# Two attention entrances of a four-block network: SyncE issues the row and stack transfers ahead of the queued DRAM writes

## The chip, the cores and the metric

The kernel runs on one core of a Trainium2 chip. The core has TensorE (PE, matrix products), VectorE (DVE), ScalarE (ACT), GpSimd (POOL) and SyncE (SP), which in this kernel does nothing but issue DMA transfers and wait for semaphores. The metric is the device time in microseconds (us) of one execution, lower is better.

## The reference, cut to what matters

```python
x = x + 0.5 * _L0_ffn_ref(_layernorm(x), ...)       # per-feature hidden layer of 16
x = x + _L0_attn_ref(_layernorm(x), ...)            # 16 heads of 8, banded bias, softmax
x = x + 0.5 * _L0_ffn_ref(_layernorm(x), ...)
x = x + 0.5 * _L1_ffn_ref(_layernorm(x), ...)       # fp4 quantised gated layer
x = x + _L1_attn_ref(_layernorm(x), ...)            # 16 causal heads over a latent of 64
x = x + 0.5 * _L1_ffn_ref(_layernorm(x), ...)
```

x is 8 batches of 256 positions by 128 features, float32. Each attention needs, for each batch and head, a 256 x 256 matrix of scores q k^T, its softmax, and the product with v.

## The kernel before, in words

Everything runs as six phases one after the other, on five instruction streams. Each stream's order is written out by hand (function `program` calls the steps), and semaphores join the streams. The change lies in the two **entrances**, the stretches where a projection phase (`proj_phase`) goes over into an attention phase (`attn_phase`): at about 40 to 90 us for the first layer's attention, and 276 to 325 us for the second layer's.

**The projection** works in four units (`p0` to `p0 + 3`), each for two batches. Per unit, q and k are split into bf16 parts (ACT lines 485 and 499, VectorE 492 or 494, GpSimd 503), and `sp_save` writes them from the tiles `q_parts` and `k_parts` to DRAM: three transfers for each of the two batches, six issues per unit, 1 MB. Semaphores `p_dram<unit><batch>` count their landing.

**The attention** works in 16 **units** of its own, each for eight heads of one batch: four slots make a quad, and a quad is two batches. So quad 0 reads what projection unit 0 wrote, quad 1 what unit 1 wrote, and so on. There are four stack buffers `qst[slot]` and `kst[slot]`. A unit needs

- its **stack**: `sp_stack` reads q and k parts back from DRAM in six issues (lines 641 and 642), and waits ahead of that until TensorE is done with the buffer (semaphore `a_t`);
- its **row**: VectorE finds the row maxima of the unit's scores, GpSimd splits them, TensorE turns them over (line 748), ACT copies them to `nmT` (line 801), and `sp_rows` copies `nmT` into the stack with one issue (line 653). The row comes with the maxima, so that the second, **shifted** pass over the scores (lines 693 to 701, in the second layer 703 and 704) gives score minus maximum.

The work is staged over units. In the unit of slot s, TensorE computes the shifted scores of s, and the plain scores of slot s + 2 (lines 672 and 673, in the second layer 675 to 679), whose maxima are wanted two units later; it starts the unit with the first pair of these plain scores. SyncE issues in the same unit the stack of slot s + 3 and the row of slot s + 1. TensorE takes its instructions in the order in which they are written. Idle products on `identb` (line 660) fill TensorE in the entrance.

In the entrance, `prefetch` issues the stacks of slots 0, 1 and 2 of quad 0, `front(0)` and `front(1)` make the scores, maxima and rows of slots 0 and 1, and `quad(0)` then runs the first four units. SyncE's order in all this is what the change rewrites. `saved(unit)` in `quad` has SyncE wait for the landing of a projection unit's writes. Stack 3 of quad 0 reads projection unit 0 only.

Of the kernel before, what the change touches and what calls it, by code (L numbers as in the profile page):

```python
# [58 lines left out]
def build(nc, A, out_d):  # L59
# [10 lines left out]
    with ctx:  # L70
# [382 lines left out]
        def proj_phase(inst, nu0, tu0, x_ready, entry, q_ready, k_ready, between):  # L453
# [147 lines left out]

            def last_save(sp):
                sp_save(sp, p0 + 3, 1)

            return dict(pe=pe_body, act=act_body, dve=dve_body, pool=pool_body, sp=sp_body, first=p0, n=4, entry=entry, ahead=ahead, last_save=last_save, opening=opening)


# [14 lines left out]

        def attn_phase(inst, last_save):
            l0 = inst == 0
            q0 = 4 * inst
# [258 lines left out]
            def unit(eng, which, qd, slot, has_prev, has_prev2, has_1, has_2, has_3, extra=lambda point: None):  # L884
# [5 lines left out]
                if which == "sp":  # L890
                    if has_3:
                        sp_stack(eng, *n3)
                    if has_1 and has_prev:
                        sp_rows(eng, *n1)
# [98 lines left out]
            def front(eng, which, slot):  # L993
# [23 lines left out]
                if which == "sp":  # L1017
                    sp_rows(eng, q0, slot)
                if which == "act":
                    act_maxT(eng, q0, slot)  # L1020
# [5 lines left out]
            def quad(eng, which, n, beside, loop=lambda qd, slot, point: None, final=lambda slot, point: None):  # L1026
# [4 lines left out]
                if n == 0:  # L1031
                    for slot in range(4):
                        unit(eng, which, q0, slot, slot > 0, slot > 1, True, True, True)
                        if slot == 0 and which == "sp":
                            last_save(eng)
                elif n == 1:
# [693 lines left out]
        def biases(eng, which):  # L1730
# [20 lines left out]
            if which == "pool":  # L1751
# [11 lines left out]
                            lambda dve, k: ffn_a["x"](dve, 2 + k, k) if k < 2 else None)  # L1763
        attn_a = attn_phase(0, proj_a["last_save"])
        ffn_b = ffn_phase(1, 8, 8, lambda t: ("a_y", 2 * (t + 1)),
# [9 lines left out]
                            lambda dve, k: step(dve, "dve", fp4_a, 15) if k == 1 else None)  # L1775
        attn_b = attn_phase(1, proj_b["last_save"])
        fp4_b = fp4_phase(1, 24, lambda t: ("a_x", t + 1),
# [3 lines left out]
        def program(eng, which):  # L1781
            def run(ph, lo, hi):
                for k in range(lo, hi):
                    step(eng, which, ph, k)
# [45 lines left out]
            def entrance(ph, at):  # L1830
# [3 lines left out]
                at["prefetch"](eng, which)  # L1834
                run(ph, 3, 4 if which == "sp" else 5)
                if which in ("pe", "dve"):
# [3 lines left out]
                elif which == "sp":  # L1840
                    at["front"](eng, which, 0)
                    run(ph, 4, 5)
                    at["front"](eng, which, 1)
                    run(ph, 5, 6)
                else:
# [197 lines left out]
```

## Time and profile before

| | us |
|---|---|
| median of 3 executions | 462.82 |
| lowest, highest | 458.14, 462.89 |
| the profiled execution, its time | 460.4 |
| its span in the profile | 458.4 |
| TensorE busy | 413.9 (90%) |
| VectorE busy | 348.8 (76%) |
| GpSimd busy | 298.3 (65%) |
| ScalarE busy | 284.8 (62%) |
| mean granted TensorE clock | 0.981 of full speed |

The span is the part of the execution that the profile covers from its first to its last instruction; 2.0 us of the execution's time lie around it. Times in the rows below count from the start of the span. In rows of SyncE ("SPq") the second number is how long the issue took on SyncE, not the transfer. The engines overlap, so their busy times don't add up to the span.

### The profile page before, as it was taken

The numbers are of one execution on the slowest core, as the hardware profiler recorded it, in microseconds if no ns is written. First come the engines' busy times: TensorE is split into PE (matmuls) and PEld (weight loads), VectorE is DVE, ScalarE is ACT, GpSimd is POOL, SyncE is SP. The second block draws the span as 40 slices with busy tenths as digits, with TensorE's granted clock in tenths as the row PEclk, the third lists the DMA queues.
The fourth block names the chain that finished last, engine by engine and source line by source line (L and its number), as shares of the span: only waits on it lengthen the run. The fifth ranks groups of instructions, "written<-read, shape, count | busy, mean of one in ns | idle before, by whom it ended". The sixth has DMA issues, their size and how long they took to land.

```text
span 458.4 us, 11229 instructions
## 1 busy us (share of the span) xinstructions
PE 413.9 (90%) x3804; PEld 265.9 (58%) x3804; DVE 348.8 (76%) x878; ACT 284.8 (62%) x523; POOL 298.3 (65%) x569
## 2 busy tenths in 40 slices
PE   8999789999999998897879888899999999887996
PEld 3555436666666654454447564567667766544674
DVE  5878766888778766996699986767788878367992
ACT  5886424666676676687886448055547575777732
POOL 5523625777777772357899647245676789779962
PEclk9999988999999999899899999989999999999999
DMA  7001876323224100000000006983343332000001
GB/s 215 2 1 49 203 211 166 107 77 85 88 73 104 55 4 1 2 0 2 0 1 2 1 1 165 234 224 93 80 104 107 82 80 56 5 0 1 23 24 46
DMA packets 31123, 31.82 MB, mean 69 GB/s; under 512 B 4953, under 2 KB 26329, under 8 KB 31074
## 3 DMA queue, kind: packets, MB, share of 16 engines
q1 hardware_dynamic: 31074, 31.18, 25.6%
q8 instruction: 28, 0.46, 0.4%
q14 instruction: 21, 0.17, 0.1%
HBM read 21.30 MB, written 9.44 MB: 67 GB/s over the span
## 4 chain that ended last, share of the span: by engine, by line
PE 49%; DVE 18%; POOL 15%; issue 8%; ACT 8%; DVEq 0%; POOLq 0%; ACTq 0%
PE psum L722 6%; ACT h_sb L349 4%; DVE nm L821 4%; POOL hq L1496 3%; PE psum L672 3%; PE psum L675 3%; PE psum L703 3%; PE psum L693 2%; PE psum L673 2%; POOL hb_v L1491 2%; PE psum L726 2%; DVE xn L240 2%; PE psum L694 2%; PE psum L660 2%; DVE nm L824 2%
## 5 line engine op out<-in xcount | busy, mean ns | idle before, releaser
L771 ACT ACTIVATE h_sb<-psum 128x1024 f32<-128x1024 f32 (+1 forms) x128 | 110.9, 914 | 45.9 <-PE psum L694 25.5
L821 DVE TENSOR_REDUCE nm<-psum 128x2 f32<-128x512 f32 x128 | 81.7, 684 | 15.0 <-PE psum L673 14.5
L824 DVE TENSOR_REDUCE nm<-psum 128x3 f32<-128x384 f32 x128 | 65.6, 551 | 10.8 <-PE psum L679 8.9
L781 POOL TENSOR_TENSOR h_sb<-h_sb,bandw 128x512 f32<-128x512 f32 x45 | 57.2, 1271 | 0.0
L246 POOL TENSOR_TENSOR rstd<-veps,mhalf 128x4 f32<-128x4 f32 (+1 forms) x29 | 27.7, 954 | 39.9 <-DVE veps L232 38.8
L722 PE MATMUL psum<-h_sb,v_b 128*32 128x256 f32 x512 | 40.9, 391 | 3.4 <-POOL h_sb L785 1.7
L785 POOL TENSOR_SCALAR_AFFINE_SELECT h_sb<-h_sb 128x512 f32<-128x512 f32 x64 | 40.8, 637 | 0.0
L672 PE MATMUL psum<-kst,qst 72*128 72x256 bf16 x128 | 33.9, 282 | 2.9 <-DMA kst<-k_dram 1.2
L858 DVE RECIPROCAL rsum<-psum 128x16 f32<-128x16 f32 x32 | 8.2, 256 | 33.7 <-PE psum L738 33.7
L675 PE MATMUL psum<-kst,qst 72*128 72x128 bf16 x128 | 29.1, 227 | 5.0 <-DVE nm L824 3.1
L673 PE MATMUL psum<-kst,qst 72*128 72x256 bf16 x128 | 33.3, 276 | 0.0
L306 PE MATMUL psum<-h_sb,dw 128*64 128x256 f32 x256 | 31.6, 392 | 0.0
L349 ACT ACTIVATE h_sb<-s_sb,pk 128x512 f32<-128x512 f32 x40 | 29.1, 802 | 0.2
L676 PE MATMUL psum<-maskqk,identb 128*128 128x128 bf16 x128 | 28.4, 222 | 0.0
L679 PE MATMUL psum<-maskqk,identb 128*128 128x128 bf16 x128 | 28.3, 221 | 0.0
L677 PE MATMUL psum<-kst,qst 72*128 72x128 bf16 x128 | 28.2, 221 | 0.0
L783 POOL TENSOR_TENSOR gate<-mhalf 128x1 f32<-128x1 f32 x64 | 12.3, 193 | 24.4 <-ACT h_sb L771 24.4
L678 PE MATMUL psum<-kst,qst 72*128 72x128 bf16 x128 | 28.0, 219 | 0.0
L1491 POOL TENSOR_TENSOR hb_v<-hh,hb_rs 128x704 f32<-128x704 f32 x16 | 22.2, 1386 | 8.5 <-DVE hb_rs L1474 8.5
L806 ACT ACTIVATE ou<-psum 128x256 f32<-128x256 f32 x32 | 12.3, 383 | 23.2 <-PE psum L728 19.4
L1195 PE MATMUL psum<-wgT,fxT 128*128 128x352 f32 x64 | 22.7, 476 | 3.8 <-ACT fxT L1266 3.8
L306 PEld LDWEIGHTS psum<-h_sb,dw 128*64 128x64 f32 x256 | 17.4, 139 | 14.2 <-issue 4.7
(256 smaller groups left out, 1176.2 us busy)
## 6 DMA issues: line engine op xcount, KB each, us to landing
qst<-q_dram SPq DMA_DIRECT2D x96, 96.0 KB
kst<-k_dram SPq DMA_DIRECT2D x96, 96.0 KB
q_dram<-q_parts SPq DMA_DIRECT2D x16, 192.0 KB, 2.6
k_dram<-k_parts SPq DMA_DIRECT2D x16, 192.0 KB, 2.8
k_dram<-k_parts SPq DMA_DIRECT2D x16, 128.0 KB, 2.9
x<-in_L_attn_x SPq DMA_DIRECT2D x4, 256.0 KB, 4.3
out_x<-x SPq DMA_DIRECT2D x4, 256.0 KB, 2.3
pk<-in_packed SPq DMA_DIRECT2D x1, 689.5 KB, 5.9
```

Source lines behind the costliest of these rows:

```text
L306: last = nc.tensor.matmul(bank[gb[par]][M * half:M * half + M, 0:256], dw2[:, p], h_sb[par][:, p, 256 * half:256 * half + 256], start=(p = ...
L349: nc.scalar.activation(h_sb[par][:, p], s_sb[par][:], ACT.Relu, bias=b1[:, p:p + 1], scale=w1[:, p:p + 1]).then_inc(sem("f_ha"), 1)
L672: nc.tensor.matmul(ps[:, 0:S], q[:, 0:P], k[:, 0:S], start=True, stop=True)
L673: last = nc.tensor.matmul(ps[:, S:2 * S], q[:, P:S], k[:, 0:S], start=True, stop=True)
L675: nc.tensor.matmul(ps[:, 0:P], q[:, 0:P], k[:, 0:P], start=True, stop=False)
L722: nc.tensor.matmul(out[c], v[:, 0], pexp[2 * g + c // 2][:, c % 2, 0:S], start=(g == 0), stop=False)
L771: nc.scalar.activation(pexp[p][:, :, 0:w], psum[:, 4 + 2 * (p % 2):6 + 2 * (p % 2), 0:w], ACT.Exp, scale=scale).then_inc(sem("a_exp"), 1)
L781: ins = nc.gpsimd.tensor_tensor(wide, wide, bandw[:].unsqueeze(1).unsqueeze(1).to_broadcast([P, 2, 2, P]), ALU.mult)
L785: ins = nc.gpsimd.affine_select(out=diag, in_=diag, compare_op=ALU.is_ge, fill=0.0, base=0, pattern=[[0, 2], [0, 2], [1, P]], channel_mult ...
L821: nc.vector.tensor_reduce(nm[slot % 2][:, HEAD[h]], bank[e].rearrange("p (t k) -> p t k", t=2), AX.X, ALU.max, negate=True).then_inc(sem(" ...
L824: nc.vector.tensor_reduce(nm3[slot % 2][:, HEAD[h]], bank[e][:, 0:3 * P].rearrange("p (t k) -> p t k", t=3), AX.X, ALU.max, negate=True).t ...
L1491: nc.gpsimd.tensor_tensor(blocks(hb_v[par][:]), hh[:, :, 0:BLK], spread(hbuf["rs"][:], NBH), ALU.mult).then_inc(sem("hv"), 1)
```

## The change

It changes SyncE's order alone, in both entrances; no other engine's instructions move, and no transfer is added or taken away. Every transfer has the same size and source as before.

- The row of slot 0 no longer stands behind the writes of projection unit 1, nor the row of slot 1 behind those of unit 2. Stack 3 goes right behind the first row.
- The writes of unit 1 go behind the row of slot 1, and SyncE then waits for their landing (`saved`), as before, at the head of quad 0.
- The writes of unit 2 go to the end of the unit of slot 1 and those of unit 3 to the end of the unit of slot 2, behind the rows of slots 2 and 3.

```diff
-            def last_save(sp):
-                sp_save(sp, p0 + 3, 1)
+            def late_save(sp, n):
+                sp_save(sp, p0 + n, n % 2)
...
                 if which == "sp":
-                    if has_3:
+                    if has_3 and has_prev:
                         sp_stack(eng, *n3)
                     if has_1 and has_prev:
                         sp_rows(eng, *n1)
...
                 if which == "sp":
                     sp_rows(eng, q0, slot)
+                    if slot == 0:
+                        sp_stack(eng, q0, 3)
...
                     for slot in range(4):
                         unit(eng, which, q0, slot, slot > 0, slot > 1, True, True, True)
-                        if slot == 0 and which == "sp":
-                            last_save(eng)
+                        if slot in (1, 2) and which == "sp":
+                            late_save(eng, slot + 1)
...
                 at["prefetch"](eng, which)
-                run(ph, 3, 4 if which == "sp" else 5)
+                if which != "sp":
+                    run(ph, 3, 5)
                 if which in ("pe", "dve"):
                     at["front"](eng, which, 0)
                     run(ph, 5, 6)
                     at["front"](eng, which, 1)
                 elif which == "sp":
                     at["front"](eng, which, 0)
-                    run(ph, 4, 5)
                     at["front"](eng, which, 1)
-                    run(ph, 5, 6)
+                    run(ph, 3, 4)
```

SyncE's queue in the first layer's entrance, from the end of the third stack on. `q_parts1` is the tile that projection unit 1 filled, the number at `qst`, `kst` and `nmT` is the buffer; a line of three dots stands for the remaining issues of the same six. Before:

```order
L642 DMA kst2<-k_dram 24x2048
L512 DMA q_dram<-q_parts1 128x3x256
...
L653 DMA qst0<-nmT0 3x16x128
L512 DMA q_dram<-q_parts2 128x3x256
...
L653 DMA qst1<-nmT1 3x16x128
L641 DMA qst3<-q_dram 24x2048
...
L512 DMA q_dram<-q_parts3 128x3x256
```

And in the changed kernel:

```order
L642 DMA kst2<-k_dram 24x2048
L653 DMA qst0<-nmT0 3x16x128
L641 DMA qst3<-q_dram 24x2048
...
L653 DMA qst1<-nmT1 3x16x128
L512 DMA q_dram<-q_parts1 128x3x256
...
L641 DMA qst0<-q_dram 24x2048
```

Both rows and the fourth stack moved up, and the writes of unit 1 stand behind them; the writes of units 2 and 3 have left this place.

SyncE's queue further on, in the units of slots 1 to 3 of the first quad. Before:

```order
L653 DMA qst2<-nmT0 3x16x128
L641 DMA qst1<-q_dram 24x2048
...
L653 DMA qst3<-nmT1 3x16x128
L641 DMA qst2<-q_dram 24x2048
L642 DMA kst2<-k_dram 24x2048
```

And in the changed kernel:

```order
L653 DMA qst2<-nmT0 3x16x128
L512 DMA q_dram<-q_parts2 128x3x256
...
L641 DMA qst1<-q_dram 24x2048
...
L653 DMA qst3<-nmT1 3x16x128
L512 DMA q_dram<-q_parts3 128x3x256
...
L641 DMA qst2<-q_dram 24x2048
```

Six write issues now stand between the third row and the stack of slot 1 of the next quad, and six between the fourth row and the stack of slot 2. The second layer's entrance is changed in the same way.

## Rows read from the trace of the kernel before

**Rows 1.** The page: the chain that ended last, by engine; a DMA issue and its landing.

```profile
PE 49%; DVE 18%; POOL 15%; issue 8%; ACT 8%; DVEq 0%; POOLq 0%; ACTq 0%
...
k_dram<-k_parts SPq DMA_DIRECT2D x16, 128.0 KB, 2.9
```

**Rows 2.** Waits of PE, 40 to 110 us: total, times, longest.

```profile
PE psum L672 <- DMA kst<-k_dram: 1.2, 1, 1.2
```

**Rows 3.** PE in order of time: start, us, instruction, in brackets the idle time before.

```profile
52.43 0.27 PE L672 MATMUL psum<-kst,qst 72*128 72x256 bf16 x1 [1.25 <-DMA kst<-k_dram]
...
286.39 0.22 PE L675 MATMUL psum<-kst,qst 72*128 72x128 bf16 x1 [1.61 <-ACT v_all L528]
...
297.56 0.30 PE L748 MATMUL psum<-identb,nmb 128*48 128x128 bf16 x1 [1.83 <-POOL nmb L850]
```

**Rows 4.** ACT in order of time: the first nmT.

```profile
60.13 0.27 ACT L801 ACTIVATE nmT<-psum 48x128 bf16<-48x128 f32 x1 [6.24 <-PE psum L748]
```

**Rows 5.** SyncE's issues in order of time, first layer's entrance: start, us on SyncE.

```profile
46.36 0.38 SPq L641 DMA_DIRECT2D qst<-q_dram  x1
...
60.42 0.76 SPq L653 DMA_DIRECT2D qst<-nmT  x1
61.23 0.44 SPq L512 DMA_DIRECT2D q_dram<-q_parts  x1
...
63.33 1.10 SPq L516 DMA_DIRECT2D k_dram<-k_parts  x2
...
65.58 0.40 SPq L641 DMA_DIRECT2D qst<-q_dram  x1
...
79.01 0.74 SPq L653 DMA_DIRECT2D qst<-nmT  x1
79.94 0.32 SPq L641 DMA_DIRECT2D qst<-q_dram  x1
...
85.79 0.76 SPq L653 DMA_DIRECT2D qst<-nmT  x1
```

**Rows 6.** SyncE's issues in order of time, second layer's entrance.

```profile
280.85 0.39 SPq L641 DMA_DIRECT2D qst<-q_dram  x1
...
299.04 0.38 SPq L641 DMA_DIRECT2D qst<-q_dram  x1
...
301.49 0.41 SPq L512 DMA_DIRECT2D q_dram<-q_parts  x1
...
303.61 2.20 SPq L516 DMA_DIRECT2D k_dram<-k_parts  x2
...
310.74 0.74 SPq L653 DMA_DIRECT2D qst<-nmT  x1
...
317.28 0.72 SPq L653 DMA_DIRECT2D qst<-nmT  x1
```

**Rows 7.** PE in order of time: the first plain scores of a unit.

```profile
74.72 0.28 PE L672 MATMUL psum<-kst,qst 72*128 72x256 bf16 x1
...
88.56 0.27 PE L672 MATMUL psum<-kst,qst 72*128 72x256 bf16 x1
...
95.61 0.28 PE L672 MATMUL psum<-kst,qst 72*128 72x256 bf16 x1
...
319.11 0.23 PE L675 MATMUL psum<-kst,qst 72*128 72x128 bf16 x1
...
325.65 0.23 PE L675 MATMUL psum<-kst,qst 72*128 72x128 bf16 x1
```

**Rows 8.** A stretch: busy us (instructions) by engine, PE clock, DMA share, GB/s.

```profile
85.00:85.50 0.50, 0.50 (x5) 0.22 (x4) 0.39 (x1) 0.20 (x2) 0.50 (x2) 1.00 0.00 0
```

**Rows 9.** The same, for three stretches of 4 us.

```profile
66.00:70.00 4.00, 4.00 (x17) 2.06 (x15) 1.92 (x4) 2.05 (x2) 2.71 (x4) 0.50 0.51 143
70.00:74.00 4.00, 4.00 (x34) 2.54 (x36) 1.81 (x4) 2.05 (x2) 1.59 (x4) 0.72 1.00 280
298.00:302.00 4.00, 4.00 (x33) 2.87 (x31) 1.47 (x3) 2.88 (x4) 0.55 (x2) 0.64 0.69 194
```

More of the change, by code:

```diff
@@ L600, in sp_body @@
                     sp_save(sp, k - 2, par)
-            def last_save(sp):
-                sp_save(sp, p0 + 3, 1)
-            return dict(pe=pe_body, act=act_body, dve=dve_body, pool=pool_body, sp=sp_body, first=p0, n=4, entry=entry, ahead=ahead, last_save=last_save, opening=opening)
+            def late_save(sp, n):
+                sp_save(sp, p0 + n, n % 2)
+            return dict(pe=pe_body, act=act_body, dve=dve_body, pool=pool_body, sp=sp_body, first=p0, n=4, entry=entry, ahead=ahead, late_save=late_save, opening=opening)
         PR = HH // 2
@@ L621, in build, with attn_phase @@
         NROW = 16
-        def attn_phase(inst, last_save):
+        def attn_phase(inst, late_save):
             l0 = inst == 0
@@ L1763, in build @@
                             lambda dve, k: ffn_a["x"](dve, 2 + k, k) if k < 2 else None)
-        attn_a = attn_phase(0, proj_a["last_save"])
+        attn_a = attn_phase(0, proj_a["late_save"])
         ffn_b = ffn_phase(1, 8, 8, lambda t: ("a_y", 2 * (t + 1)),
@@ L1775, in build @@
                             lambda dve, k: step(dve, "dve", fp4_a, 15) if k == 1 else None)
-        attn_b = attn_phase(1, proj_b["last_save"])
+        attn_b = attn_phase(1, proj_b["late_save"])
         fp4_b = fp4_phase(1, 24, lambda t: ("a_x", t + 1),
```

## The prediction

> **What bounds the kernel now.** I read the chain that ended last first: it is made of TensorE (49%), VectorE (18%) and GpSimd (15%), with no DMA step in it [rows 1]. So SyncE, the only engine that the change touches, matters just where someone waits for one of its transfers. Next I asked who waited for a DMA. In the whole first entrance and the units behind it (40 to 110 us) TensorE waited for one once, for 1.2 us [rows 2], and the order of time shows that this was for the first stack of all, in use from 52.43 us after an idle 1.25 us [rows 3]. It is issued ahead of everything that the change moves. In the second entrance the same place stands as a wait of 1.61 us put down to ACT [rows 3].
>
> Then I looked whether SyncE is late with the two rows, since the change takes writes away from in front of them. ACT makes the first nmT from 60.13 to 60.40 us and SyncE issues its row at 60.42 [rows 4, 5]. The second row of this layer and both rows of the other one stand in the same way, within 0.03 us of the end of their nmT (three more pairs like this one). The writes that stand ahead of the rows are issued while SyncE would be waiting.
>
> That leaves the fourth stack. It is issued from 65.58 us on [rows 5] and the scores that read it begin at 74.72 us [rows 7], 9.1 us later. How long a stack takes I get from three places. SyncE began the first stack at 46.36 us and TensorE, idle and waiting, began at 52.43: 6.07 us [rows 3, 5]. In the second layer that is 280.85 to 286.39: 5.54 us [rows 3, 6]. And the stack whose issue begins at 79.94 [rows 5] has no traffic left from 85.0 us on [rows 8]: 5.0 us, without the receipt. I take 5.5 us from the first issue of a stack to its use, between 5.0 and 6.07. So the fourth stack was there by 71.1 us, 3.6 us early. In the second layer units follow each other by 6.54 us (325.65 less 319.11), so the need for the fourth stack, two units ahead of 319.11, is at 306.0; its first issue is 299.04 [rows 6, 7], so it was there by 304.5, 1.5 us early.
>
> **The change part by part.**
>
> (a) Rows ahead of the writes: nothing was late, so nothing is won: 0 us.
>
> (b) The fourth stack ahead by some 4.4 us (it follows the first row, at 61.2 us instead of 65.58): that only adds slack, 0 us. It is worth more only if the first unit runs faster than in this trace (rival 3).
>
> (c) The second unit's writes go behind both rows. Six issues took 3.20 us with nothing in the way (61.23 to 64.43 [rows 5]) and 4.32 us (301.49 to 305.81 [rows 6]) behind a stack. They now start right behind the second row and the fourth stack, at about 65.5 us, and are issued by 69 to 70. Behind them SyncE stands at the wait for their landing, a median of 2.9 us from an issue [rows 1]: until 72 to 73 us. Queued behind that wait is only the first stack of the next quad. This one waits for the first unit's four shifted pairs anyway, and is needed one whole unit after the fourth stack, at about 81.5 us. With 5.5 us for the stack there are 3 us to spare, and in the second layer some 2 us: 0 us.
>
> (d) The third unit's writes go behind the third row. Before, the row at 79.01 us was followed at 79.94 by the next stack (slot 1 of the second quad) [rows 5]; now six issues stand between: 79.01 + 0.74 for the row, + 3.20 for the writes = 83.0 us, and the stack is usable at 83.05 + 5.5 = 88.55 us. Its need is 88.56 [rows 7]. The 3.1 us of slack that it had are used up: 0 us in the middle, 0.55 at the late end (6.07). In the second layer the units are shorter, 6.54 us against 7.05 (95.61 less 88.56), and the same sum goes over: row at 310.74 + 0.74, + 3.20 = 314.7; + 5.5 = 320.25 against the need at 319.11 [rows 6, 7]: 1.15 us late, with ends at 0.65 and 1.7. TensorE takes its work in order, so it stands still for that time, with everything that hangs on it.
>
> (e) The fourth unit's writes go behind the fourth row, and are issued while a stack is under way, so I take the middle of 3.20 and 4.32 us, 3.76. First layer: row from 85.79 to 86.5 [rows 5], writes to 90.3, stack usable at 95.8 (94.8 to 97.0) against 95.61 [rows 7]: 0.2 us (0 to 1.4). Second layer: row 317.28 + 0.72 = 318.0, writes to 321.8, stack at 327.3 (326.2 to 328.4) against the old need of 325.65 [rows 6, 7]. This is a lateness against the old time of the trace and holds the 1.15 us of (d) in it: 1.65 us in all, between 0.65 and 2.75. After this unit no more writes are inserted, the next stack waits for its own unit, and no further lateness arises; the loop's wait for the third and fourth unit's writes finds them landed.
>
> (f) The fourth row now stands right behind a stack that is still in flight. Its price is not in the trace, where a row follows a stack by 3 us or more in these units. It is needed about 0.5 us behind that stack's own first use, so it costs nothing if it lands together with the stack's last bytes, and some 0.5 us if it takes its turn behind them. I take 0 and leave the rest to the range. None of (c) to (f) can go below nothing: nobody waits for an earlier landing.
>
> Sum: 0.2 + 1.65 = 1.85 us, with ends 0.65 and 4.15 (1.4 + 2.75). On the profiled execution that is 460.4 + 1.85 = 462.25 us. The four executions shown of before (458.14, 462.82, 462.89 and the profiled 460.4) have a mean of 461.06, 0.66 above the profiled one; since the median of three sits in the upper of two clusters 4.7 us apart, I carry the sum over to that mean: **462.9 us**, which is the median of before within 0.02%. A measurement of this kernel can tell about 1% (4.6 us) from no change.
>
> **Where a page speaks against this.** The issue of six writes takes 3.20 us [rows 5], and a stack 5.5 us from first issue to use, so SyncE's own time is over half of a transfer's here. The Trainium skill, "DMA: Bandwidth & Descriptors", section "Issuing engines are not separate DMA queues", says that the time to initiate a DMA is usually small relative to the DMA itself. By that rule (d) and (e) would cost nearly nothing and the sum would be 0, which is rival 1; the trace doesn't agree, with its 3.20 us of issuing.
>
> **The rivals.**
>
> 1. The moved writes stay hidden. If a stack with an empty queue ahead of it takes 5.0 us and SyncE's six issues 3.2, the first layer loses nothing and the second 0.65 us. If TensorE gets that back from the short waits for VectorE that it has in each unit of that layer, nothing is left: 461.1 us. For it: the early ends of my own terms. Against it: the 6.07 and 5.54 us at the two places where someone really waited.
>
> 2. Slower by over 1%: the stalls pull the clock down. The granted clock was 0.50 from 66 to 70 us and 0.64 from 298 to 302 [rows 9], so at the lower of its two levels (1.2 of 2.4 GHz) for a part or all of these slices, the latter after TensorE had stood idle for 1.83 us; it didn't fall after the idle 1.25 and 1.61 us [rows 3]. The price from the slices is (0.50 + 0.28) x 4 = 3.1 us for the first fall and 0.36 x 4 = 1.4 us for the second. The rival decides if one new stall on a stack reaches some 1.8 us, which needs the late end of (d) in the second layer. Then 4.15 + 1.4 to 3.1 gives 466.6 to 468.3 us. The Trainium skill, "TensorE: Matmul & The Clock Gate", section "HAM oscillation — how this bites in real kernels", tells of a kernel whose DMA waits had it start each burst at the low clock. Against it: the new stalls are two, of about 1.15 and 0.5 us, both under the lengths after which it held.
>
> 3. A gain. The first unit of each entrance ran partly at the low clock in this trace. In an execution in which the clock holds, the second unit starts 1.4 us sooner in the second layer, at 304.6, and there the fourth stack (304.5 to 305.1) is late by up to 0.5 us; the change takes that away. With (d) and (e) at nothing that is 460.6 us. A gain of 1% has no mechanism that I can see in this trace; only the spread of single executions makes one.
>
> **How the numbers follow.** The forecast (0.65 to 4.15 us lost) has a chance of 0.58, rival 1 has 0.22, rival 2 has 0.12, rival 3 has 0.08. The range goes from 459.0 (rival 3 with the spread of the executions) to 466.9 (all terms at their late ends and the short fall of the clock). Slower by over 1% means over 467.4: most of rival 2 and the upper tail of the forecast by the executions' spread, 0.12. Faster by over 1% means under 458.2, where one execution of before lay: 0.08. The rest, 0.80, is within 1%.
>
> **What would show it.** In the profile of the changed kernel: rows issued at the same distance from ACT's nmT as now; the fourth stack's first issue right behind the first row; six write issues right behind the third and fourth row, and the first issues of the stacks of slots 1 and 2 some 3.3 to 3.8 us later than now. TensorE should show new waits for kst or qst at the scores (line 675) of the fourth unit and the one behind it in the second layer, of 0.7 to 2.8 us in all, and next to none in the first layer. I am wrong if TensorE shows no wait there, or if it stands at the shifted scores (line 703) in place of line 675, which would make (f) the price and not (d), or if the granted clock falls at about 320 us.

## The result, and the profile after

| | before | changed |
|---|---|---|
| median of 16 executions each | 462.63 us (457.51 to 465.33) | 468.64 us (463.21 to 478.43) |
| ratio, 95% interval | | 1.0132 (1.0091 to 1.0172) |
| profiled execution, time | 460.4 us | 466.33 us |
| its span | 458.4 us | 464.3 us |
| its mean granted clock | 0.981 | 0.973 |

The change makes the kernel 1.3% slower, some 6 us; forecast were 462.9 us and at most 466.9. The ratio leaves out executions that the run's own record marks as disturbed, some of the changed kernel's slowest among them; over all 16 of each, the means are 469.01 and 461.65 us.

The page of the changed kernel, busy times and the chain that ended last:

```profile
PE 416.1 (90%) x3804; PEld 268.2 (58%) x3804; DVE 348.7 (75%) x878; ACT 284.7 (61%) x523; POOL 299.1 (64%) x569
...
PE 47%; DVE 18%; POOL 14%; issue 8%; ACT 7%; DMA 2%; SPq 2%; DVEq 0%; POOLq 0%; ACTq 0%
```

The engines did the same work. What is new stands in the chain: 2% DMA and 2% SyncE's queue, where [rows 1] had neither.

Where TensorE waits for a DMA, in the waits of the second layer's entrance (270 to 340 us):

```profile
PE psum L675 <- DMA kst<-k_dram: 2.1, 1, 2.1
```

In order of time on TensorE, the first scores at both new waits:

```profile
87.14 0.28 PE L672 MATMUL psum<-kst,qst 72*128 72x256 bf16 x1 [1.13 <-DMA kst<-k_dram]
...
319.27 0.23 PE L675 MATMUL psum<-kst,qst 72*128 72x128 bf16 x1 [2.12 <-DMA kst<-k_dram]
...
323.90 1.08 PE L722 MATMUL psum<-h_sb,v_b 128*32 128x256 f32 x8
```

At 319.27 us the fourth unit of the second layer begins, after 2.12 us in which TensorE stood idle for its stack. Before, the unit began at 319.11 us [rows 7] without such a wait, and in the changed kernel it would have been due at 317.15. The last row is a sign of what came next: this group of eight products takes 0.64 us elsewhere in the trace and 1.08 here.

SyncE in order of time ahead of that wait (start, duration, what it issues):

```profile
308.72 0.75 SPq L653 DMA_DIRECT2D qst<-nmT  x1
309.51 0.44 SPq L512 DMA_DIRECT2D q_dram<-q_parts  x1
310.00 1.04 SPq L516 DMA_DIRECT2D k_dram<-k_parts  x2
311.08 0.49 SPq L512 DMA_DIRECT2D q_dram<-q_parts  x1
311.61 1.09 SPq L516 DMA_DIRECT2D k_dram<-k_parts  x2
312.74 1.36 SPq L641 DMA_DIRECT2D qst<-q_dram  x1
...
315.78 0.36 SPq L642 DMA_DIRECT2D kst<-k_dram  x1
316.18 0.73 SPq L653 DMA_DIRECT2D qst<-nmT  x1
```

The row at 308.72 answers to the one at 310.74 in [rows 6], and the six writes behind it end at 312.70: 3.19 us from the first, as [rows 5] had them. The stack begins at 312.74 and is used at 319.27, so it took 6.53 us. Its first issue alone held SyncE for 1.36 us (in [rows 5] and [rows 6] a first issue of a stack is over in 0.32 to 0.45 us), and the next row could start only at 316.18. The stack behind the next six writes, at 320.20 us, had a first issue of 0.57 us. Single slow issues are not new, though: the kernel before has them too, some where only stacks and rows are in the queue:

```profile
331.64 1.55 SPq L642 DMA_DIRECT2D kst<-k_dram  x1
```

In the changed kernel, the nmT of the row at 316.18 had been there since 315.24:

```profile
314.98 0.26 ACT L801 ACTIVATE nmT<-psum 48x128 bf16<-48x128 f32 x1
```

so the row is 0.94 us late behind SyncE's own issues (in the first layer 0.67 us). TensorE's waits show none for it: the unit that needs it was itself waiting for its stack until 319.27.

The clock, by stretches (length, busy time of PE, PEld, DVE, ACT and POOL, granted clock, DMA share, GB/s), changed kernel:

```profile
62.00:66.00 4.00, 2.22 (x15) 1.33 (x16) 2.08 (x4) 0.27 (x1) 0.88 (x4) 1.00 0.61 154
66.00:70.00 4.00, 3.87 (x34) 2.53 (x33) 2.76 (x5) 2.61 (x3) 2.88 (x5) 1.00 0.70 195
316.00:320.00 4.00, 1.88 (x33) 1.33 (x31) 1.80 (x6) 0.78 (x2) 3.09 (x9) 0.95 0.87 224
320.00:324.00 4.00, 3.88 (x35) 3.09 (x36) 2.48 (x5) 1.51 (x2) 1.52 (x4) 0.50 0.86 233
324.00:328.00 4.00, 4.00 (x35) 2.73 (x35) 1.03 (x4) 2.05 (x4) 0.68 (x2) 0.50 0.14 41
328.00:332.00 4.00, 4.00 (x49) 2.62 (x47) 2.68 (x7) 0.99 (x2) 1.83 (x8) 0.77 0.61 148
```

Right behind the new stall, from 319.6 us, TensorE was at its lower level (1.2 GHz) for 10.2 us. Before, the longest such stretch was 6.8 us, at 65.4 us [rows 9], the others 2.8 to 3.4. In this execution of the changed kernel that one did not occur: the clock held from 66 to 70 us, and it held from 298 to 302 us too, where it stood at 0.64 before [rows 9]. Neither stretch lies behind a late stack.

The times at which the rows are issued, changed less before, tell where the 5.9 us of span came from:

| place | before | changed | difference |
|---|---|---|---|
| third row, first layer | 79.01 | 76.30 | -2.71 (the clock held here) |
| fourth row | 85.79 | 83.72 | -2.07 |
| the next | 93.11 | 91.69 | -1.42 |
| last row of the layer's attention | 164.23 | 162.85 | -1.38 |
| third row, second layer | 310.74 | 308.72 | -2.02 (the clock held here) |
| fourth row | 317.28 | 316.18 | -1.10 |
| the next | 323.83 | 326.04 | +2.21 |
| the one behind it | 330.37 | 334.59 | +4.22 |
| 45 us on | 376.95 | 381.19 | +4.24 |

In the first layer 1.3 us are lost in two units, and the lucky clock hides them. In the second layer 6.24 us are lost in three units and nothing is made good: 2.12 us are the stall itself, and 4.1 us go with the 10.2 us at the lower clock behind it. The rest of the 5.9 us is a stretch at the lower clock at 401.5 us.

### The profile page after: what moved, and what is told of

Its sections match the earlier page's. It is cut to its first block, busy times and chain, and to the rows that moved or that the text cites. A ratio compares the mean times of both kernels' runs of the same rounds, so it can differ in the third digit from the quotient of the medians.

```text
span 464.3 us, 11229 instructions
## 1 busy us (share of the span) xinstructions
PE 416.1 (90%) x3804; PEld 268.2 (58%) x3804; DVE 348.7 (75%) x878; ACT 284.7 (61%) x523; POOL 299.1 (64%) x569
## 4 chain that ended last, share of the span: by engine, by line
PE 47%; DVE 18%; POOL 14%; issue 8%; ACT 7%; DMA 2%; SPq 2%; DVEq 0%; POOLq 0%; ACTq 0%
PE psum L722 6%; POOL hq L1498 4%; DVE nm L821 4%; PE psum L672 3%; ACT h_sb L349 3%; PE psum L675 3%; PE psum L703 2%; PE psum L693 2%; POOL hb_v L1493 2%; DVE xn L240 2%; PE psum L673 2%; PE psum L306 2%; PE psum L726 2%; PE psum L694 2%; DVE nm L824 2%
## 5 line engine op out<-in xcount | busy, mean ns | idle before, releaser
L722 PE MATMUL psum<-h_sb,v_b 128*32 128x256 f32 x512 | 42.2, 402 | 3.5 <-POOL h_sb L785 1.7
L672 PE MATMUL psum<-kst,qst 72*128 72x256 bf16 x128 | 33.3, 278 | 4.2 <-DMA kst<-k_dram 2.5
L675 PE MATMUL psum<-kst,qst 72*128 72x128 bf16 x128 | 29.4, 230 | 7.1 <-DVE nm L824 2.8
L673 PE MATMUL psum<-kst,qst 72*128 72x256 bf16 x128 | 32.7, 272 | 0.0
L677 PE MATMUL psum<-kst,qst 72*128 72x128 bf16 x128 | 28.7, 224 | 0.0
L678 PE MATMUL psum<-kst,qst 72*128 72x128 bf16 x128 | 28.5, 222 | 0.0
L1197 PE MATMUL psum<-wgT,fxT 128*128 128x352 f32 x64 | 24.0, 501 | 3.8 <-ACT fxT L1268 3.8
L703 PE MATMUL psum<-qst,kst 75*128 75x256 bf16 x128 | 26.3, 283 | 0.0
```

Source lines behind the costliest of these rows:

```text
L672: nc.tensor.matmul(ps[:, 0:S], q[:, 0:P], k[:, 0:S], start=True, stop=True)
L673: last = nc.tensor.matmul(ps[:, S:2 * S], q[:, P:S], k[:, 0:S], start=True, stop=True)
L675: nc.tensor.matmul(ps[:, 0:P], q[:, 0:P], k[:, 0:P], start=True, stop=False)
L703: nc.tensor.matmul(ps[:, 0:S], k[:, 0:P], q[:, 0:S], start=True, stop=True)
L722: nc.tensor.matmul(out[c], v[:, 0], pexp[2 * g + c // 2][:, c % 2, 0:S], start=(g == 0), stop=False)
```

## The experiments

A single execution depends so much on where the clock happens to fall that medians alone mislead. Over all executions whose clock is on record (86 different ones of before, 6 to 16 of each other kernel), a straight line with one common slope ties time to mean granted clock: 3.49 us for 0.01 of clock, with 0.09 of standard error and 1.28 us left over. So each kernel gets a **level**: its time at clock 0.98, from the mean of all its executions. It tells what the order of work costs apart from the clock. The line is a correlation; that the clock makes the time is what the longer product groups at 1.2 GHz show, not the fit.

| kernel | ratio to before | interval | ratio of all | mean clock | level |
|---|---|---|---|---|---|
| before | | | | 0.979 | 461.06 (0.14) |
| changed | 1.0132 | 1.0091 to 1.0172 | 1.0159 | 0.967 | 464.51 (0.34) |
| x1_front | 1.0007 | 0.9966 to 1.0048 | 0.9993 | 0.981 | 461.56 (0.37) |
| x2_late | 1.0142 | 1.0057 to 1.0227 | 1.0194 | 0.962 | 464.40 (0.55) |
| x3_behind | 1.0042 | 0.9994 to 1.0090 | 1.0068 | 0.978 | 463.88 (0.37) |
| x4_fill | 1.0032 | 0.9968 to 1.0096 | 1.0112 | 0.978 | 465.93 (0.37) |
| x5_small | 1.0066 | 1.0016 to 1.0115 | 1.0102 | 0.976 | 463.78 (0.37) |
| x6_full | 1.0158 | 1.0088 to 1.0228 | 1.0188 | 0.968 | 464.88 (0.53) |
| x7_fourth | 1.0087 | 1.0044 to 1.0131 | 1.0133 | 0.970 | 463.34 (0.35) |
| x8_third | 1.0120 | 1.0068 to 1.0171 | 1.0174 | 0.970 | 465.16 (0.37) |
| x9_warm | 0.9944 | 0.9906 to 0.9982 | 0.9914 | 0.991 | 461.23 (0.38) |
| x10_frontwarm | 1.0009 | 0.9960 to 1.0059 | 0.9981 | 0.984 | 462.14 (0.37) |
| x11_split | 1.0071 | 1.0025 to 1.0118 | 1.0103 | 0.977 | 465.31 (0.37) |

"Ratio of all" compares the means of all executions, with those of before taken in the same series. In brackets the standard error of the level, in us. The changed kernel's mean, 469.01 us, is 7.7 us above that of before over all series (461.27): 3.45 in its level, and 4.3 for a mean clock that is 0.0123 lower. Since the lower level is half the higher, 0.0123 is some 11 us more at 1.2 GHz per execution (an estimate: 2 x 0.0123 x 465), about the one stretch of 10.2 us that the profile shows.

### x1_front and x2_late: the two halves of the change apart

x1_front moves the second row and the fourth stack ahead of the third unit's writes, and issues the third and fourth unit's writes behind the second row, ahead of the second quad's first stack. The second unit's writes stay ahead of the first row. x2_late leaves all of this as before and moves only the writes of the third and fourth unit to their late places. So neither moves the second unit's writes, part (c) of the prediction.

```diff
 x1_front
-                    if has_3:
+                    if has_3 and has_prev:
...
+                    if slot == 0:
+                        sp_stack(eng, q0, 3)
...
                     at["front"](eng, which, 0)
+                    at["front"](eng, which, 1)
                     run(ph, 4, 5)
-                    at["front"](eng, which, 1)
-                    run(ph, 5, 6)
 x2_late
-                        if slot == 0 and which == "sp":
-                            last_save(eng)
+                        if slot in (1, 2) and which == "sp":
+                            last_save(eng, slot + 1)
...
                     at["front"](eng, which, 0)
-                    run(ph, 4, 5)
                     at["front"](eng, which, 1)
-                    run(ph, 5, 6)
```

Expected of x1_front:

> The front of the change alone: the fourth stack right behind the first row and the third unit's writes behind the second row, but the second unit's writes stay ahead of the first row, and all writes are issued before the second quad's first stack. Theory A (the cost is the writes that stand ahead of the stacks of slots 1 and 2 of the second quad): no wait of TensorE for kst in the units of the first quad, ratio to before 0.997 to 1.003. Theory B (the early fourth stack, in flight together with a row, or the rows' new place costs): the loss is here too, ratio 1.008 or more. Theory C (chance falls of TensorE's clock): the ratio can be anything from 0.99 to 1.01, with the low clock at places that don't follow a wait for kst.

Expected of x2_late:

> The late writes alone: the rows and the fourth stack stand as in the kernel before, the third and fourth unit's writes stand behind the third and fourth row. Theory A: the waits of TensorE for kst are the same as in the changed kernel, about 1.1 us in the first layer and 2.1 us in the second, and the ratio to before is 1.009 to 1.017. Theory B: no more than 0.3% slower than before. Theory C: waits as in A, but a ratio of no more than 1.007 (the waits' own 3.2 us), since the falls of the clock are not theirs.

Measured: a median of 460.70 us beside 461.8 for before (ratio 1.0007), against 471.34 us (ratio 1.0142). The late writes alone bring a loss as large as the whole change's; from the early rows and the early fourth stack no gain can be seen. One part of the expectation failed: x1_front's TensorE does wait for a stack in the second layer, the first one of the second quad, which there stands behind all the writes:

```profile
314.67 0.23 PE L675 MATMUL psum<-kst,qst 72*128 72x128 bf16 x1 [1.19 <-DMA kst<-k_dram]
```

The clock held behind this wait, and the ratio stayed at that of before. x2_late's profile has TensorE wait for stacks in both layers, longer than the 1.1 us expected in the first (and once more there, for 0.49 us at 87.56):

```profile
96.31 0.28 PE L675 MATMUL psum<-kst,qst 72*128 72x256 bf16 x1 [1.65 <-DMA kst<-k_dram]
...
326.04 0.23 PE L678 MATMUL psum<-kst,qst 72*128 72x128 bf16 x1 [2.15 <-DMA kst<-k_dram]
```

After each of the two the clock stood at 0.50 for 10.2 us, from 98.6 and from 327.3 us.

### x3_behind: the same writes behind the stack, ahead of the next row

```diff
+                    extra("stacked")
...
+                        def behind(point, slot=slot):
+                            if point == "stacked" and slot in (2, 3):
+                                late_save(eng, slot)
-                        if slot in (1, 2) and which == "sp":
-                            late_save(eng, slot + 1)
...
```

> The changed kernel with the third unit's writes one place on, behind the stack of slot 1 and ahead of the fourth row, and the fourth unit's behind the stack of slot 2: as many bytes and issues in the same units, but none of them ahead of a stack that is waited for next. Theory A: the waits for kst of 1.1 and 2.1 us are gone, at most 0.3 us is left at the rows or at the stack of slot 3, ratio to before 0.997 to 1.003. If the load on the DMA engines in these units costs, and not the place in the queue, the ratio stays at 1.008 or more. Theory B: ratio stays at 1.013.

Measured: ratio 1.0042, level 2.8 us above before. It came out as neither theory said. In the second layer the stall did not vanish, it changed its object:

```profile
321.74 0.28 PE L703 MATMUL psum<-qst,kst 75*128 75x256 bf16 x1 [1.18 <-DMA qst<-nmT]
...
329.38 0.28 PE L703 MATMUL psum<-qst,kst 75*128 75x256 bf16 x1 [0.93 <-DMA qst<-nmT]
```

The nmT of the first was made by 317.94 us and its row issued at 319.45, behind the writes. Two of these write issues (line 516, at 315.18) took 2.56 us together, against 1.05 for the same pair elsewhere. In the first layer there is a wait of 1.16 us for a stack at 101.36. So six write issues are not free at this place either. Here the clock held behind all these waits, and the ratio is two thirds smaller than the changed kernel's; most of that is clock, for the level is only 0.6 us lower than the changed kernel's, with an error of 0.5.

### x4_fill: the changed kernel, with TensorE kept busy during the stall

Eight products on a constant tile, whose result is not used, stand ahead of the fourth unit of the second layer.

```diff
+                    if not l0 and isinstance(qd, int) and (qd, slot) == (q0, 3):
+                        wait(eng, "a_exp", PR * 4 * qd + PR * slot - 1)
+                        pe_idle(eng, 8, 4)
```

> The changed kernel, and in the second layer eight idle products of 512 columns (1.7 us at the full clock) ahead of the scores of the fourth unit, where TensorE stood idle for 2.12 us. They fill most of the wait and lengthen nothing that isn't waited for. Theory A with the clock as its second half: the stall stays (kst lands no sooner), but the clock no longer falls behind it; the 10.2 us at the lower clock in the second layer are gone or cut to a third, some 3 us less than the changed kernel, ratio to before 1.004 to 1.009. Theory C: the clock falls as often as in the changed kernel, ratio 1.013 or more.

Measured: ratio 1.0032, mean clock 0.978 in place of 0.967. The median is 466.99 us, and over all executions the ratio is 1.0112, so the kernel is still slower than before. By stretches:

```profile
316.00:320.00 4.00, 3.87 (x46) 2.33 (x39) 2.00 (x5) 0.55 (x2) 2.66 (x8) 1.00 0.97 251
320.00:324.00 4.00, 3.75 (x54) 2.68 (x52) 2.38 (x6) 2.46 (x6) 1.53 (x4) 1.00 0.75 202
```

The unit began at 318.52 us, 10.39 us behind its third row at 308.13 (10.55 in the changed kernel), so the stack was no earlier; the idle products filled the wait, and the clock stayed at full. Over the executions the mean clock rose by 0.010, with an error of 0.0044, and the mean time fell by 2.2 us, with an error of 1.7. So the fall at 320 us goes with TensorE's standing idle and not with the late stack as such, as far as one profile and a clock difference of 2.4 errors can show it. But the level rose by 1.4 us over the changed kernel's, with an error of 0.5, so the filler is not free; from what, the runs do not tell.

### x5_small and x6_full: is it the issuing or the bytes?

Both start from the kernel before and issue six more writes of the same parts, to scratch tensors, at the two late places. In x5_small these are small pieces (8 KB each), in x6_full the full 1 MB. The lines below are x5_small's; x6_full has whole tiles in the same places. Neither changes what the kernel computes.

```diff
+            def extra_save(sp, n):
+                for e in range(2):
+                    el = 2 * (n - 2) + e
+                    sp.dma_start(q_scr[inst, el:el + 1, 0:1].rearrange("a i d h t -> (a d h) i t")[0:16], parts[0][n][0:16, e, 0:1]).then_inc(sem("dup"), 16)
+                    for lo in (0, NPART):
+                        sp.dma_start(k_scr[inst, el:el + 1, lo:lo + 1].rearrange("a j d h t -> (a d h) j t")[0:16], parts[1][n][0:16, e, 0:1]).then_inc(sem("dup"), 16)
...
+                        if slot in (1, 2) and which == "sp":
+                            last_save[1](eng, slot + 1)
```

Expected of x5_small:

> The kernel before, whose own writes all stay where they are, plus six small transfers (8 KB each, to a DRAM tensor that nobody reads) at each of the two late places: SyncE's issuing time without the bytes. If the issuing time alone makes the stacks late (my sum of part d, with 5.5 us for a stack), the wait for kst in the second layer is 0.6 to 1.2 us and the time at an equal granted clock 0.5 to 1.5 us over the kernel before. If the bytes in the DMA queue are the larger part, it is under 0.5 us; if issuing is all of it, 3 us as in the changed kernel.

Expected of x6_full:

> The same with six transfers of the full size of a unit's writes (1 MB) at each of the two late places: issuing time and bytes. Theory A: waits for kst as in the changed kernel, 2 us in the second layer and 1 in the first, 3 to 4 us over the kernel before at an equal granted clock and more falls of the clock, ratio 1.009 to 1.018. If the changed kernel's loss has another source (the order in the front part, the fourth stack), this one loses less than 1 us.

Measured: ratios 1.0066 and 1.0158. x6_full alone reproduces the whole loss of the change, from a kernel in which everything else stands where it did (its writes come on top, so it moves 2 MB more per entrance). On TensorE and SyncE, x5_small:

```profile
314.21 0.43 SPq L607 DMA_DIRECT2D q_scr<-q_parts  x1
...
316.08 1.77 SPq L609 DMA_DIRECT2D k_scr<-k_parts  x2
317.89 0.39 SPq L650 DMA_DIRECT2D qst<-q_dram  x1
...
323.31 0.23 PE L684 MATMUL psum<-kst,qst 72*128 72x128 bf16 x1 [1.45 <-DMA kst<-k_dram]
```

and x6_full:

```profile
312.99 0.44 SPq L607 DMA_DIRECT2D q_scr<-q_parts  x1
...
316.23 1.36 SPq L650 DMA_DIRECT2D qst<-q_dram  x1
...
322.70 0.23 PE L684 MATMUL psum<-kst,qst 72*128 72x128 bf16 x1 [2.06 <-DMA kst<-k_dram]
```

Behind small writes the stack's first issue takes 0.39 us and the stack 5.42 us from there to its use (323.31 less 317.89); behind 1 MB it takes 1.36 us and 6.47 us (322.70 less 316.23). But the slow issue is not the bytes' own. x5_small has one too, only a place earlier, inside its small writes: the pair at 316.08 took 1.77 us, where the same pair took 0.87 at 314.69. Counted from the first extra write to the use of the stack it is 9.10 us (323.31 less 314.21) against 9.71 (322.70 less 312.99), so the bytes add 0.6 us in these two profiles. The stall of 1.45 us stands without them: issuing is the larger part, by level 2.7 of 3.8 us; the 1.1 us between these two levels have an error of 0.7. The wait and the level of x5_small lie above what was expected of the issuing time alone (0.6 to 1.2 and 0.5 to 1.5 us). In the first layer x5_small has no wait for a stack, x6_full one of 1.29 us at 89.86.

Both stalls were followed by the lower clock, x5_small's too:

```profile
322.00:326.00 4.00, 2.69 (x32) 2.28 (x33) 2.26 (x6) 1.51 (x2) 2.64 (x8) 0.87 0.31 78
326.00:330.00 4.00, 4.00 (x35) 2.38 (x33) 1.38 (x3) 1.04 (x3) 0.84 (x3) 0.50 0.42 93
```

### x7_fourth and x8_third: one unit's writes late, not both

x7_fourth leaves the third unit's writes where they were and moves only the fourth's, behind the fourth row. x8_third moves only the third's, behind the third row.

```diff
 x7_fourth
-                        if slot == 0 and which == "sp":
-                            last_save(eng)
+                        if slot == 2 and which == "sp":
+                            last_save(eng, 3)
 x8_third
                         if slot == 0 and which == "sp":
-                            last_save(eng)
+                            last_save(eng, 3)
+                        if slot == 1 and which == "sp":
+                            last_save(eng, 2)
...
                     at["front"](eng, which, 0)
-                    run(ph, 4, 5)
                     at["front"](eng, which, 1)
-                    run(ph, 5, 6)
```

Expected of x7_fourth:

> The kernel before with the fourth unit's writes alone moved behind the fourth row, the rest as before. If the late stacks share one lateness (the second is late against the old time, not on top of the first), one late write costs nearly what two cost: a wait for kst of about 2 us at the first unit of the second quad in the second layer and up to 1 us in the first, ratio 1.006 to 1.014. If each late write has a price of its own and they add, it is half of the changed kernel's, ratio 1.004 to 1.008 and a wait of 1 us.

Expected of x8_third:

> The kernel before with the third unit's writes alone moved behind the third row; the fourth unit's stay ahead of the second quad's first stack. The mirror of the one before: shared lateness gives a wait for kst of about 2 us at the fourth unit of the second layer and about 1 us in the first, ratio 1.006 to 1.014; prices that add give half, 1.004 to 1.008.

Measured: levels 2.3 and 4.1 us over before; both late together, as in the change, 3.45. The waits are one of 2.43 us (x7_fourth, second layer only) and one of 2.13 us with 0.79 us in the first layer (x8_third):

```profile
332.49 0.23 PE L675 MATMUL psum<-kst,qst 72*128 72x128 bf16 x1 [2.43 <-DMA kst<-k_dram]
```

```profile
323.19 0.29 PE L675 MATMUL psum<-kst,qst 72*128 72x128 bf16 x1 [2.13 <-DMA kst<-k_dram]
```

The sum of the two levels would be 6.4 us, so the two late places share one lateness: once the fourth unit has waited, everything behind it is later too, and the fourth unit's writes find room. That x8_third lies 0.65 us above the changed kernel, with an error of 0.5, is left open.

### x9_warm and x10_frontwarm: the entrance kept busy

x9_warm is the kernel before with eight products on a constant tile ahead of the turning of the second row in both entrances, where TensorE stood idle for 1.83 us before [rows 3] in the second layer, and for 1.77 us in the first. x10_frontwarm is x1_front with the same line.

```diff
                     if slot == 1:
+                        pe_idle(eng, 8)
                         pe_maxT(eng, q0, 1)
```

Expected of x9_warm:

> The kernel before with eight idle products of 512 columns (1.7 us at the full clock) in both entrances, at the place where TensorE stands idle for 1.8 us ahead of the second row's turning. It tests whether TensorE's idle time is what the falls of the clock follow, without any late stack. If so, the mean granted clock over the executions rises by 0.003 to 0.008 and the time falls by 1 to 3 us, ratio 0.994 to 0.999. If the falls follow something else (load as such, chance), clock and time stay: ratio 0.999 to 1.003.

Expected of x10_frontwarm:

> The front part alone (x1_front: fourth stack right behind the first row, all writes ahead of the second quad's first stack) with the same eight idle products. If the early fourth stack is worth something once the first unit runs at the full clock (rival 3 of the prediction), this is faster than x9_warm by 0.5 us or more at an equal granted clock; otherwise the two agree within 0.4 us, ratio 0.994 to 1.000.

Measured: x9_warm 457.16 us beside 461.07 for before, ratio 0.9944 (0.9906 to 0.9982). It is faster than both kernels. By stretches:

```profile
66.00:70.00 4.00, 3.87 (x36) 2.57 (x34) 2.60 (x5) 2.63 (x3) 3.04 (x5) 1.00 0.49 137
298.00:302.00 4.00, 4.00 (x48) 2.75 (x50) 3.12 (x6) 2.27 (x4) 2.87 (x9) 1.00 0.87 226
```

The two stretches that stood at 0.50 and 0.64 in [rows 9] are at 1.00. Its level is that of before (461.23 to 461.06): all that is won is clock, 0.991 for 0.979, more than the 0.003 to 0.008 expected. x10_frontwarm tests rival 3: if the clock holds, the fourth stack should be late and the early issue should help. It does not: x9_warm, whose clock held in both entrances, shows no wait of TensorE for a DMA between 290 and 345 us, so its fourth stack was not late; and x10_frontwarm's level is 462.14, 0.9 us above x9_warm's, with an error of 0.5, where a gain of 0.5 us or agreement within 0.4 was expected. In its second layer the first stack of the second quad is issued at 306.90 us, and at 302.80 in x9_warm, because all the writes stand ahead of it, and its unit waits for it for 1.06 us, as in x1_front.

### x11_split: the changed kernel with half doses

Three writes at a time: half of the third unit's ahead of the first unit, the rest behind the third row, the fourth's in halves behind the fourth and the next.

```diff
+                        late_save(eng, 2, [0])
-                        if slot in (1, 2) and which == "sp":
-                            late_save(eng, slot + 1)
+                        if slot in (1, 2, 3) and which == "sp":
+                            late_save(eng, *((2, [1]), (3, [0]), (3, [1]))[slot - 1])
```

> The changed kernel with half doses: the third unit's writes go half ahead of the first unit of the quad and half behind the third row, the fourth unit's half behind the fourth row and half behind the row after it. Ahead of each waited-for stack stand three issues (1.6 us) and 0.5 MB instead of six and 1 MB. By the sum with the 6.5 us that a stack took behind 1 MB and 5.4 behind small transfers, so about 6.0 here, the stack of slot 1 is usable 1.6 + 6.0 = 7.6 us behind the row's end; it was needed 7.6 us behind it in the second layer (319.11 less 311.48) and 8.8 us in the first: no wait in the first layer, 0 to 0.5 us in the second, at an equal granted clock 0 to 1 us over the kernel before, ratio 1.000 to 1.004. If the price doesn't hang on the dose but on any write between row and stack, it stays at 2.5 us or more.

Measured: ratio 1.0071, level 465.31, 4.3 us above before. The expectation failed, and the level is one for which it had named the other reading, a price that doesn't hang on the dose. The three writes ahead of the first unit push the second quad's first stack, and the stall comes one unit earlier:

```profile
306.28 0.46 SPq L641 DMA_DIRECT2D qst<-q_dram  x1
...
311.96 0.23 PE L675 MATMUL psum<-kst,qst 72*128 72x128 bf16 x1 [1.73 <-DMA kst<-k_dram]
...
336.88 0.23 PE L675 MATMUL psum<-kst,qst 72*128 72x128 bf16 x1 [1.14 <-DMA kst<-k_dram]
```

The half dose behind the row after the fourth makes a second wait, the one at 336.88 us; in the first layer there is one of 0.95 us at 101.78. So the doses made new places for stalls, and this run does not tell what half a dose costs at the old ones.

## Why the prediction was wrong

- **(a) and (b), rows and fourth stack ahead, 0 us: right.** x1_front is equal to before (1.0007, within 0.5%). Rival 3 needed a late fourth stack once the clock holds; x9_warm has the clock and no such wait, and x10_frontwarm gains nothing.
- **(c), second unit's writes behind both rows: right for this change.** SyncE's waits show the new one for their landing, 1.8 us once in the first layer, and TensorE waits for no stack there. It was not tested alone. The 2 to 3 us of room are soon used up: x11_split, with three more writes ahead of that stack, stalls there for 1.73 us, and x1_front and x10_frontwarm for 1.19 and 1.06 us.
- **(d), third unit's writes ahead of a stack: the right place, line 675 of the fourth unit in the second layer, and undersized. This is the step that failed.** "0 us in the middle" in the first layer became 1.13 us, and 1.15 us in the second became 2.12. The six issues were right (3.19 for 3.20). What was wrong is the "5.5 us from the first issue of a stack to its use": it was 6.84 us in the first layer (80.30 to 87.14) and 6.53 in the second. That accounts for the whole miss of (d). In the second layer the stack was due 8.43 us behind its row's issue (317.15 less 308.72; 8.37 in the trace of before) and was used 10.55 us behind it, where my sum had 9.5. In the first layer it was due 9.71 us behind (86.01 less 76.30; 9.55 in my sum) and used at 10.84. The units ran 2 to 2.7 us sooner than in the trace of before, but the rows with them, so that did not add to it.

  Over all the profiles, a stack that TensorE waited for took 5.42 us behind small writes (x5_small), 5.8 to 6.0 behind twelve full ones (x1_front and x10_frontwarm), and 5.8 to 7.1 right behind six full ones (x2_late: 6.22, 7.08 and 6.58; x4_fill: 6.43 and 6.26; x6_full: 5.84 and 6.47; x7_fourth: 6.87; x8_third: 6.50 and 6.76). My late end of 6.07 was in fact measured with traffic, for the stack at 46.36 us [rows 5] stands 0.12 us behind the end of six write issues (the last pair from 45.15 us, for 1.09); it still was too low. Part of the excess goes with a slow issue, 1.36 us on SyncE in place of 0.45. I had priced such an issue for the writes of (e), and not for a stack. But single issues of some 1 to 2 us turn up in every kernel's entrances, before and small writes included, and x2_late's 7.08 us hold none: why a stack takes 6.5 to 7 us here is open. x8_third (0.79 us), x2_late (0.49 and 1.65), x4_fill (0.72) and x6_full (1.29) show first-layer stalls too.
- **(e), fourth unit's writes, shared with (d): right in its form.** x7_fourth costs 2.3 us alone, both together no more than x8_third alone. The size is off as in (d).
- **(f), a row behind a stack in flight, 0 us: right for the change, where TensorE shows no wait for a row in either entrance; but the row waits for SyncE's issuing.** 316.18 us against an nmT of 315.24 is a term that I did not have: with six writes and a slow first issue ahead, SyncE is still issuing the stack when the row is due. In the profile of the changed kernel the late stack hides it. x3_behind shows what it becomes when it is larger: 1.18 us at line 703.
- **Rival 2, the stalls pull the clock down, "decides if one new stall on a stack reaches some 1.8 us": this is what happened, and it had a chance of 0.12.** The prediction's own sign of being wrong, a fall of the clock at about 320 us, came at 319.6. The chance was too low because the stall was sized by (d), and because 1.8 us is no threshold: stalls on a stack of 1.45 (x5_small), 1.65 (x2_late), 1.73 (x11_split), 2.06, 2.12, 2.13, 2.15 and 2.43 us were all followed by the lower clock, while the shorter waits for a stack or a row behind the first unit, thirteen of 0.49 to 1.29 us, were not. Nor does the length alone decide: ahead of the second layer's first scores TensorE stood idle for 1.61 to 2.14 us in 12 of the 13 profiles (2.43 in x3_behind), and in 11 of these the clock held; behind the idle 1.77 and 1.83 us of the two entrances it fell in some profiles and held in others; and behind the wait for the very first stack at 52 us, 0.99 to 1.59 us, it fell in four profiles and held in nine. The rival's price of 1.4 to 3.1 us per fall came from falls of 3.4 and 6.8 us; the falls behind these stalls lasted 10.2 us in five cases, 20.5 in two and 23.8 in one. Its time, 466.6 to 468.3 us, ends just under the measured 468.64. By the fit, the lower mean clock costs 4.3 us on the mean, more than the 3.45 of the stalls and shifts themselves. x4_fill (clock back with the stack still late) and x9_warm (clock raised with nothing else changed) are the experiments for it.
- **The sum:** 1.85 us forecast; 3.45 in the level and 4.3 in the clock. The range ended at 466.9 because its end took "the short fall of the clock"; its own terms add up to 466.6 (461.06 + 4.15 + 1.4).

## What to carry to other kernels

Price a DMA that is moved ahead of another one by its issuing time on the queue's engine and by its bytes in the queue, and use a duration that was taken behind such a queue: here 5.4 us behind small writes became 5.8 to 7.1 behind 1 MB. Where TensorE is 90% busy, a new wait of 1.5 to 2.5 us is not priced by its length alone: count the stretch at the lower clock behind it, and ask of every forecast of "1 us late" what happens if it is 2. And look for idle stretches of this length that are already there: eight idle products in each of two of them made this kernel 0.56% faster. Compare kernels at equal clock as well as by their medians, and look at the mean of all executions: x4_fill has a ratio of 1.0032 by one count and 1.0112 by the other.

## What the hardware did that I had not expected

- Idle stretches of TensorE of 1.45 to 2.43 us on a stack were all followed, up to 2.3 us later, by 10 to 24 us at 1.2 GHz; the falls in the profile of before lasted 2.8 to 6.8 us. A fall of 10.2 us needs no late stack, though. In the first layer's entrance of x1_front, x5_small, x7_fourth and x8_third one began between 63.6 and 68.0 us, where no stack was late; x1_front's:

```profile
66.00:70.00 4.00, 4.00 (x17) 2.37 (x16) 1.54 (x3) 2.05 (x2) 1.80 (x4) 0.50 0.74 203
```

  Of 11 profiles with the same idle 1.83 us at line 748 in the second layer, six have a fall behind it (before among them) and five not (the changed kernel among them). What sets the length of a fall was not tried.
- Executions of one kernel spread over 6 to 17 us, and nearly all of it goes with the mean granted clock: 3.49 us for 0.01, 1.28 us left over.
- An issue on SyncE that mostly takes 0.36 to 0.55 us takes 1 to 2 us now and then, once or a few times in each entrance and at changing places: on the first issue of the stack behind 1 MB of writes (1.34 and 1.36 us in the changed kernel), but also on the fifth of a stack (1.51 us at 86.17 in x5_small) or where only stacks and rows were queued (1.55 at 331.64 before). What brings it on is open.
- The Trainium skill, "DMA: Bandwidth & Descriptors", section "Issuing engines are not separate DMA queues", calls the time of initiating usually small relative to the DMA itself. For one transfer the trace agrees (0.36 to 0.55 us beside 2.4 to 2.9 us to landing for a write), for six in a row it doesn't: they take 3.2 us beside a stack's 5.4, and adding small ones alone costs 2.7 us of level.
- Why x4_fill's level lies 1.4 us above the changed kernel's, although its longest wait for a stack in the second layer is down to 0.64 us (one unit on, at 325.75), is open.
